# Reordering tile 0's first two diffusion steps ahead of tile 1's coefficients, with two passes on ScalarE and one coefficient built by a copy and an adding DMA

## What is computed

```python
g  = relu(bn(dwconv(h, wg)));  g1 = relu(bn(dwconv(h, wg1)));  gy, gx = sobel(h)
Dx = 1/(gy*gy/4 + 1);  Dy = 1/(gx*gx/4 + 1)
ux = 0.5*(roll(g,1,w) - roll(g,-1,w));  vy = 0.5*(roll(g1,1,c) - roll(g1,-1,c))
Ax, Ay, Bx, By, E = g*DT, g1*DT, Dx*DT, Dy*DT, (ux+vy)*DT
D  = 1/(1 + 2*Bx + 2*By)
for _ in range(5):
    prev = h
    h = D*((1-2*Bx-2*By)*h0 - 2*E*h + (-Ax+2*Bx)*roll(h,1,w) + (Ax+2*Bx)*roll(h,-1,w)
           + (-Ay+2*By)*roll(h,1,c) + (Ay+2*By)*roll(h,-1,c)) + D*2*DT*s
    h0 = prev
```

## Time and profile before

| | us |
|---|---|
| median of 3 runs (lowest, highest) | 278.0 (277.66, 278.8) |
| the profiled execution | 277.91 |
| its span | 276.1 |
| VectorE busy | 247.2 |
| TensorE busy (weight loads beside it) | 233.6 (209.6) |
| ScalarE busy | 133.8 |
| POOL busy | 16.8 |

### The profile page before, as it was taken

The page is one execution under the profiler, slowest core; times in us unless marked ns, Lnnn a source line. Parts: engine busy times, 40 slices in busy tenths (PEclk is TensorE's granted clock), DMA queues, the critical chain, the costliest instruction groups (busy, mean ns, idle before and its releaser), DMA issues.

```text
span 276.1 us, 5235 instructions
## 1 busy us (share of the span) xinstructions
PE 233.6 (85%) x2276; PEld 209.6 (76%) x2276; DVE 247.2 (90%) x196; ACT 133.8 (48%) x207; POOL 16.8 (6%) x36
## 2 busy tenths in 40 slices
PE   0137999999959999279999999999999987889793
PEld 0136889989925588279989999898989986767683
DVE  3799999999999989999998999999999989886821
ACT  3294776879860054702623425160603246917743
POOL 2000000003310201101000101010101000000000
PEclk9999999999979999959999999999999999999999
DMA  6950000005998771990700334248610030000124
GB/s 213 350 116 0 0 4 6 2 0 112 199 205 253 152 152 38 209 209 2 154 0 2 76 78 94 61 116 190 129 26 1 0 138 17 2 0 0 62 93 152
DMA packets 7190, 24.94 MB, mean 90 GB/s; under 512 B 2816, under 2 KB 3328, under 8 KB 5120
## 3 DMA queue, kind: packets, MB, share of 16 engines
q0 software_dynamic: 2304, 14.68, 26.6%
q1 hardware_dynamic: 4720, 9.61, 10.6%
q10 hardware_dynamic: 144, 0.33, 0.4%
HBM read 6.79 MB, written 2.10 MB: 32 GB/s over the span
## 4 chain that ended last, share of the span: by engine, by line
DVE 54%; PE 27%; issue 9%; ACT 7%; DMA 1%; DVEq 0%; ACTq 0%
DVE ring L918 24%; DVE coef L653 8%; PE psum L1180 8%; PE psum L1170 6%; ACT coef L380 5%; PE psum L1257 5%; DVE first_two L1004 4%; PE psum L1117 3%; PE psum L1087 3%; DVE state L729 2%; DVE coef L964 1%; DMA bn<-in_norms 1%; DVE ring L722 1%; DVE hi_s L734 1%; DVE gsum L687 1%
## 5 line engine op out<-in xcount | busy, mean ns | idle before, releaser
L918 DVE TENSOR_TENSOR ring<-coef,state 128x2048 f32<-128x2048 f32 x51 | 113.5, 2286 | 2.1 <-PE psum L1180 1.9
L1180 PE MATMUL psum<-mats,ring 128*128 128x128 f32 x816 | 96.6, 278 | 9.6 <-DVE ring L918 9.5
L1180 PEld LDWEIGHTS psum<-mats,ring 128*128 128x128 f32 x816 | 91.4, 144 | 13.3 <-DVE ring L918 12.9
L380 ACT ACTIVATE state<-psum 128x1024 f32<-128x1024 f32 x36 | 35.1, 1028 | 74.3 <-PE psum L1180 60.2
L653 DVE SCALAR_TENSOR_TENSOR coef<-coef 128x2048 f32<-128x2048 f32 x16 | 36.4, 2290 | 0.7 <-issue 0.2
L380 ACT ACTIVATE coef<-coef 128x2048 f32<-128x2048 f32 (+1 forms) x10 | 17.6, 1783 | 10.1 <-DMA coef<-coef 9.9
L1257 PE MATMUL psum<-hi,dense_m 128*128 128x512 f32 (+1 forms) x54 | 20.0, 379 | 0.9 <-ACT coef L380 0.9
L1139 PEld LDWEIGHTS psum<-coef,state 32*128 32x128 f32 x672 | 19.4, 187 | 1.4 <-issue 1.3
L380 ACT ACTIVATE coef<-psum 128x512 f32<-128x512 f32 (+2 forms) x23 | 17.5, 766 | 5.4 <-PE psum L1117 4.3
L1139 PE MATMUL psum<-coef,state 32*128 32x64 f32 x672 | 20.0, 271 | 0.0
L1257 PE MATMUL psum<-lo,dense_m 128*128 128x512 f32 (+1 forms) x54 | 19.5, 369 | 0.0
(11 more groups left out here) (133 smaller groups left out, 280.4 us busy)
## 6 DMA issues: line engine op xcount, KB each, us to landing
first_two<-coef POOLq DMA_DIRECT2D x7, 1024.0 KB, 8.5
coef<-coef POOLq DMA_DIRECT2D x5, 1024.0 KB, 8.8
coef<-in_x SPq DMA_DIRECT2D x2, 1024.0 KB, 6.0
coef<-in_wide_taps SPq DMA_DIRECT2D x3, 384.0 KB, 7.6
ring<-in_x SPq DMA_DIRECT2D x2, 512.0 KB, 6.0
ring<-in_x SPq DMA_DIRECT2D x1, 1024.0 KB, 10.3
coef<-coef SPq DMA_DIRECT2D x1, 1024.0 KB, 7.6
out<-coef SPq DMA_DIRECT2D x2, 512.0 KB, 3.1
```

Of the source, the lines that this page charges most:

```text
L380: return nc.scalar.activation(dst, src, func, **kw)
L918: V.tensor_tensor(wc(ring[:, slot, :]), wc(coef[:, t, a, :]), h_at(t, k, dw, dc), ALU.mult)\
L1180: ins = mm(slot_ap(name)[:, (j % 8) * 128:(j % 8) * 128 + 128], src[:, j * 128:j * 128 + 128], ident, is_transpose=True, start=first and j ...
```

## The change

VectorE now makes source(0) and runs step (0,0) before newton(1), with divergence_added after its second product, denominator(1) after its third and the request for the output norm after its fourth; step (1,0) stands before over_rows(1), over_channels(1), divergence_taken and source(1). The ring is used in the order 0, 2, 1. On TensorE tile 1's convolutions stand before its Sobel groups, divergence(0) before the sum of step (1,0) and divergence(1) before that of step (0,1); the source of a first step is added after the fourth product. On ScalarE are now the rounding of tile 0 (`split_hi(0)`) and the regrouping of tile 1 (`reorder(1)`, after the scaling). `over_rows(1)` makes AXM alone; ScalarE writes -0.5 times it to a free state plane (`source_at[0]`), and POOL adds that to AXP by a DMA. In POOL's program the DMA is put in between first_source(0) and other_rows(1). Some of tile 0's passes are cut in halves; in the tail the second rsqrt of the last norm stands before relu_dense(0,0). `coef` becomes two tensors.

```diff
@@ job_table
-             ("gy_0_1", 2), ("gx_0_0", 3), ("var_1", 1), ("gx_0_1", 0), ("cv_0_0", 2), ("cv_0_1", 3), ("cv_0_2", 0),
...
+             ("gy_0_1", 2), ("var_1", 0), ("gx_0_0", 3), ("alpha", 1), ("gx_0_1", 0), ("cv_0_0", 2), ("cv_0_1", 3),
...
@@ POOL
             def other_rows(t):
-                pool.wait_ge(axp_ready, t + 1)
+                if t:
+                    pool.wait_ge(axp_full, 16)
+                else:
+                    pool.wait_ge(axp_ready, 1)
...
             other_channels(0)
             pool.wait_ge(sb_begun, 16)
             pool.wait_ge(column_part, 2)
-            pool.dma_start(coef[:, 1, 2, :], coef[:, 1, 5, :], accum_op=ALU.add).then_inc(sb_added, 16)
+            pool.dma_start(coef[1][:, 2, :], coef[1][:, 5, :], accum_op=ALU.add).then_inc(sb_added, 16)
             first_source(0)
+            pool.wait_ge(half_ready, 1)
+            pool.dma_start(coef[1][:, AXP, :], source_at[0], accum_op=ALU.add).then_inc(axp_full, 16)
             other_rows(1)
@@ ScalarE
+            def split_hi(t):
+                act.wait_ge(s_ready, t + 1)
+                copy(wc(s_parts[t][0][:, :]), h_at(t, 0)).then_inc(s_hi, 1)
+            def reorder(t):
+                act.wait_ge(s_ready, t + 1)
+                copy(s_grouped[t].rearrange("p (g a w e) -> p a w g e", e=2, a=CP, w=W),
+                     h_at(t, 0).rearrange("p w (a g e) -> p a w g e", a=CP, e=2)).then_inc(s_grouped_ready, 1)
...
                 keep_turned(k, t, 1)
+                if (k, t) == ORDER[1]:
+                    act.wait_ge(ayp_ready, 2)
+                    wait_job(act, "dv_1_1")
+                    copy_s(1)
...
                 wrap(t, k + 1, halo_ready)
                 if (k, t) == ORDER[0]:
-                    act.wait_ge(ayp_ready, 2)
-                    wait_job(act, "dv_1_1")
-                    copy_s(1)
                     source_of(0)
-                if (k, t) == ORDER[1]:
+                    d_of(1)
+                    a0_of(1)
+                    act.wait_ge(axm_ready, 1)
+                    copy(source_at[0], coef[1][:, AXM, :], scale=-0.5).then_inc(half_ready, 1)
+                if (k, t) == ORDER[2]:
                     source_of(1)
             rsqrt_first(128, BT)
             normalise(0)
             upper_half(0)
             relu_bn_out(1, 0)
             relu_bn_out(1, 1)
+            rsqrt_first(128, BT)
             relu_dense(0, 0)
-            rsqrt_first(128, BT)
@@ VectorE
             over_rows(0)
...
-            denominator(1)
             over_channels(0)
+            source(0)
+            step(0, 0, ((1, divergence_added), (2, lambda: denominator(1)), (3, ask_out)))
             newton(1)
+            out_norm()
             across_rows(1)
             across_columns(1)
...
-            step(0, 0)
+            step(1, 0)
             over_rows(1)
             over_channels(1)
             divergence_taken()
             source(1)
-            step(1, 0)
@@ TensorE
-            for g in range(2):
-                for h in range(2):
-                    sobel(1, g, h)
...
             depthwise(1, 0)
             depthwise(1, 1)
-            divergence(0)
-            divergence(1)
+            for g in range(2):
+                for h in range(2):
+                    sobel(1, g, h)
             last = None
             for k, t in ORDER:
...
+                if last is not None and last[0] < STEPS - 1 and last[1] == t:
+                    back_to_natural(*last)
+                if (k, t) == ORDER[1]:
+                    divergence(0)
+                if (k, t) == ORDER[2]:
+                    divergence(1)
                     back_to_natural(*last)
...
                 take_sums(t, k)
+                if k == 0:
+                    add_products(t, k, ((3, lambda: add_source(t, 0, False)),), True)
+                    last = (k, t)
+                    continue
```

More of the change, by code:

```diff
@@ L326, in first_source @@
                 pool.wait_ge(s_copied[t], 1)
-                pool.dma_start(first_two[t][:, :], coef[:, t, FS, :], accum_op=ALU.add).then_inc(first_full[t], 16)
+                pool.dma_start(first_two[t][:, :], source_at[t], accum_op=ALU.add).then_inc(first_full[t], 16)
             pool.wait_ge(e_made, 3)
@@ L572, in take_out @@
                 wait_job(act, name)
-                frees(copy(part(coef[:, t, 4, :], t, h), part_slot(name, t, h)), name)
+                frees(copy(part(coef[t][:, 4, :], t, h), part_slot(name, t, h)), name)
             def keep_turned(k, t, h):
@@ L837, in both_diffusivities @@
                 dve.wait_ge(column_part, t + 1)
-                signal(V.tensor_tensor(coef[:, t, 2, :], coef[:, t, 4, :], coef[:, t, 5, :], ALU.add), sb_ready, t + 1)
+                for h in range(2):
+                    V.tensor_tensor(half(coef[t][:, 2, :], h), half(coef[t][:, 4, :], h), half(coef[t][:, 5, :], h), ALU.add)\
+                        .then_inc(sb_ready, 1)
             def taken_out(t):
@@ L847, in over_rows @@
                 taken_out(t)
-                dve.wait_ge(d_ready, t + 1)
                 dve.wait_ge(row_part, t + 1)
                 dve.wait_ge(column_part, t + 1)
-                then(stt(coef[:, t, AXM, :], gN[t], 2.0, coef[:, t, 0, :], ALU.mult, ALU.mult))
-                stt(coef[:, t, AXP, :], coef[:, t, AXM, :], -0.5, coef[:, t, AXP, :], ALU.mult, ALU.add)\
+                if t:
+                    dve.wait_ge(d_ready, 3)
+                    signal(stt(coef[t][:, AXM, :], gN[t], 2.0, coef[t][:, 0, :], ALU.mult, ALU.mult), axm_ready, 1)
+                    return
+                else:
+                    for h in range(2):
+                        dve.wait_ge(d_ready, h + 1)
+                        done = mark(stt(half(coef[t][:, AXM, :], h), half(gN[t], h), 2.0, half(coef[t][:, 0, :], h),
+                                        ALU.mult, ALU.mult))
+                    done()
+                stt(coef[t][:, AXP, :], coef[t][:, AXM, :], -0.5, coef[t][:, AXP, :], ALU.mult, ALU.add)\
                     .then_inc(axp_ready, 1)
@@ L1118, in sobel @@
                                      sobel_m[:, m, :], part[:, frm * C:(frm + count) * C],
-                                     start=(i == 0 and part is s_parts[0]), stop=(i == last and part is s_parts[1]),
+                                     start=(i == 0 and n == 0), stop=(i == last and n == 1),
                                      skip_group_check=True)
-                ins.then_inc(pe_job, 1)
+                if passes[-1] == 1:
+                    ins.then_inc(pe_job, 1)
             def depthwise(t, h):
@@ L1210, in add_products @@
                     pe.wait_ge(product, summed[0] + 1)
-                    ins = add_turned(t, k, ring[:, summed[0] % RING, :], first and i == 0, i == count - 1)
+                    ins = add_turned(t, k, ring[:, -summed[0] % RING, :], first and i == 0, i == count - 1)
                     summed[0] += 1
@@ L1286, in _ @@
             pe.wait_ge(sobel_m_ready, 4)
-            sobel(0, 0, 0)
-            sobel(0, 0, 1)
+            for n in range(2):
+                sobel(0, 0, 0, (n,))
+                sobel(0, 0, 1, (n,))
+            group_var(1)
             sobel(0, 1, 0)
-            group_var(1)
+            pe.wait_ge(kept_ready, 1)
+            small("alpha", 2, ones[:, :], wred[:, 3:5])
             sobel(0, 1, 1)
```

253 lines of the change are left out of this document (134 added, 119 removed), and 4 rows, old and new, of the table early.

## The result

| | before | after |
|---|---|---|
| median (lowest, highest), us | 278.4 (277.66, 278.98) | 311.63 (311.44, 313.59) |
| ratio of medians, 95% interval | | 1.121 (1.116 to 1.127) |
| span of the profiled execution | 276.1 | 309.8 |
| VectorE busy | 247.2 | 242.3 |
| TensorE busy | 233.6 | 238.7 |

What follows compares the result with a forecast made beforehand. VectorE was taken as the bound, busy 247.2 of 276.1 us, with TensorE nearly as long. Step (1,1) 34.2 later and 1.3 off the tail gave 309.0 of span, plus 1.8 made 310.8; forecast 310, range 300 to 316.

Steps and rivals of the forecast that it cites:

- wait for the divergence: VectorE in step (0,0), before divergence_added: waits 1.8 us for the divergence's negative part, landing at 79.8; bounds 0 and 3.
- SP's copy lands after: SP's copy after across_rows(1), ahead of POOL's addition and source DMA: lands 7.6 us after issue, as in the earlier trace.
- source lands: Source of step (0,0), behind SP's copy and POOL's addition: lands 19.8 us after across_rows(1) ends at 99.3, at 119.1.
- source and last product: TensorE ending step (0,0): 16 transposes each at the 1.2 GHz level, 2.3 and 2.2 us instead of 1.8, until 123.6.
- wait in step (0,1): Last product of step (0,1) waits 2 us for the second late DMA, until 170.4.
- waits in step (2,0): VectorE at the start of step (2,0) waits 5.6 us for a ring place, instead of 0.69 in the trace.
- tail: Last norm's second rsqrt ahead of relu_dense(0,0) on ScalarE: saves 1.3 us, between 0 and 1.6.
- main term: Before step (1,0): the source, late in POOL's queue behind SP's copy and an addition, leaves VectorE idle 26.2 us.
- four late DMAs: POOL's other_rows(1), other_channels(1), first_source(1) and step (1,0)'s kept DMA follow in a row, landing at 164.0, 168.2, 172.5, 176.8.
- first rival: POOL's late DMAs run beside each other, so the last five us of waits vanish: 305, or 302; chance within the 0.80.
- rival in which the source isn't held back: Source leaves POOL before the copy, no wait at 101.6, tile 1's late DMAs still follow each other: about 281 us; chance 0.03.
- faster: Source not held back and the transfers hidden too, so a 3.4 us gain and 1.3 of tail stay: 273 us; chance 0.03.

Runs made afterwards that it cites:

- one moved line: In POOL's program of the changed kernel, first_source(0) put ahead of the wait for SP's copy and the addition to tile 1's plane 2: 288.26 us, ratio to before 1.033.

## Why the prediction was right, point by point

| step | predicted | measured |
|---|---|---|
| step (0,0) starts | 73.6 | 72.46 |
| wait for the divergence | 1.8 | 2.74 |
| across_rows(1) ends, SP copies | 99.3 | 99.30 |
| SP's copy lands after | 7.6 | 4.5 |
| source lands | 119.1 | 116.0 |
| source and last product | 4.5 | 6.2 |
| step (1,0) starts | 127.8 | 126.54 |
| VectorE's wait there | 26.2 | 25.07 |
| ring wait in step (1,0) | 3.3 | 2.72 |
| wait for divergence(1) | 1.5 | 1.23 |
| wait in step (0,1) | 2 | 3.67 |
| waits in step (2,0) | 5.6 | 6.38 |
| step (1,1) starts | 189.0 | 189.94 |
| tail | -1.3 | -1.4 |
| device time | 310 | 311.63 |

The main term held by mechanism and size: one moved line takes 23.4 us off. The reading that carried it is that a DMA is as late as what stands ahead of it in its queue, even if its own operand is long ready.

Two terms of the source's chain were mis-sized and cancelled in part. SP's copy took 4.5 us: the row of 7.6 in the earlier trace rows had an addition of tile 0 beside it, and alone a plain copy was faster than any 1 MB transfer there. By the Trainium skill, DMA: Bandwidth & Descriptors, "Anatomy of one DMA — SWDGE (gpsimd) path", 1 MB issued by GpSimd takes an estimated 4.4 us; SP's plain copy is near that, though it leaves from another engine. For GpSimd's own adding DMA, alone, the trace doesn't agree: 7.0 for the addition here, as in the earlier trace rows. Source and last product took 6.2 us instead of 4.5, because I took the rate behind 5.57 us of idling from a stretch of one us (7 transposes); 16 transposes took 3.67. Together these two are -3.1 and +1.7, the rest of -1.3 being rounding. The DMA that ended the wait was first_two<-state, issued at 104.63, and not first_two<-coef near 107, since source(0) is written to a free state plane.

Part of the nearness of 310 to 311.63 is luck: step (1,0) starts 1.3 us earlier than forecast, and the waits behind it add up to 14.0 us instead of 12.4. The early start of step (0,0), 1.1 us, is no such case: the negative part of the divergence landed at 79.6 as forecast (79.8), so VectorE's wait for it grew by 0.9.

The four late DMAs went in a row, as put: landing at 161.5, 168.0, 172.8 and 177.7 against 164.0, 168.2, 172.5 and 176.8. The first rival (transfers beside each other, 305) is thereby wrong.

The rival in which the source isn't held back was put at about 281; that kernel took 288.26. Its shape was right, and it was mis-sized by the slower first Sobel group (2 us), by waits of 1.6 and 1.2 us in and behind step (1,0) that it left out, and by late waits that were 2.6 us longer. So even without the queue's order the change loses, and the chance I gave to "faster" rested on transfers that nothing hides.

Of the gain on VectorE, 4.9 us, little arrived: the far coefficient's 2.3 cost 8.7 in DMAs that follow each other, and the rounding's 1.2 came to nothing. The regrouping is the one move that helps in the new order, and not by its 2.3 us alone: without it TensorE has the gap of 2.77 us ahead of tile 1's convolution, and five of six executions were 11.8 us slower. In the old order the same move came with the stop of TensorE and was slower, so its worth there stays open.

## What to carry to other kernels

When work is moved ahead, every queue that feeds it must be read as a program: a DMA stands behind waits for work that is now later, and the engine that runs ahead then waits for its own queue. A pass taken off the busiest engine by way of an adding DMA is not free if other DMAs follow it in the same queue; such DMAs of 1 MB landed 4.8 to 6.5 us apart here. And a gap of some us on TensorE must be priced with the clock behind it, above all in front of small matmuls.

## What the runs showed of the hardware that was not expected

- The granted clock fell to the 1.2 GHz level behind gaps of 1.0 (changed kernel, 65.5 us), 2.75 and 2.77 us in the convolutions, and behind 3.1 us ahead of the divergence. Followed by Sobel groups or transposes it was back within 3 to 7 us; followed by the 32-row convolution matmuls it stayed low until these were over: 58 to 81 us in one kernel, 72 to 85 in another, with 10.52 us for 192 instead of 5.59. The length of a gap didn't decide it alone: behind 2.60 us, at 86.3 in the changed kernel, the clock stayed at 1.00.
- With 26 transposes of a constant in a gap of 3.1 us the clock stayed at 1.00, and they paid for themselves: 277.49 to 275.46 us.
- A plain 1 MB copy within SBUF, issued by SP, took 4.5 us alone; an adding one, issued by GpSimd, 7.0 alone, and 13.1, 17.0 and 21.4 behind one, two and three others.
- TensorE stood still for 1.0 and 2.75 us in the middle of a convolution with no wait in the trace. The cause is open.
